# TensorE's attention programs written out without a loop, and two of ScalarE's copies placed ahead of an exponential

## What is computed

```python
x = x + _L0_xattn_ref(_layernorm(x), ctx, ...)   # 8 heads of 128
x = x + _L0_ffn_ref(_layernorm(x), ...)          # ternary mixture of experts
x = x + _L1_xattn_ref(_layernorm(x), ctx, ...)   # 16 heads of 8, with biases
x = x + _L1_ffn_ref(_layernorm(x), ...)
x = x + _L2_xattn_ref(_layernorm(x), ctx, ...)   # 16 heads of 64
x = x + _L2_ffn_ref(_layernorm(x), ...)
x = x + _L3_xattn_ref(_layernorm(x), ctx, ...)   # 16 heads of 64
x = x + _L3_ffn_ref(_layernorm(x), ...)
```

## Time and profile before

| | |
|---|---|
| runs of the kernel, median | 3998.56 us (3996.25 to 4007.36, 3 runs) |
| the profiled execution's own time | 3976.25 us |
| its span, first to last instruction | 3974.5 us |
| mean granted TensorE clock | 0.929 |
| busy: PE, PE's weight loads | 91%, 76% |
| busy: DVE, ACT, POOL | 62%, 46%, 28% |
| DMA queue of kind "instruction" | 305 packets, 5.00 MB |

### The profile page before, as it was taken

One profiled execution on the slowest core, in us unless ns is written; L12 is line 12 of the kernel. 1 busy time (PEld: TensorE's weight loads), 2 busy tenths in 40 slices (PEclk: granted clock), 3 DMA queues, 4 the chain that ended last, 5 costly groups with the idle time before them and its releaser, 6 DMA issues. The chain is left out here.

```text
span 3974.5 us, 110071 instructions
## 1 busy us (share of the span) xinstructions
PE 3612.0 (91%) x44952; PEld 3024.5 (76%) x44952; DVE 2445.7 (62%) x5145; ACT 1821.4 (46%) x3060; POOL 1102.7 (28%) x814
## 2 busy tenths in 40 slices
PE   4999599998989788699999989979999997999999
PEld 3888588886778654488878867768788886888888
DVE  5777555554444499766665657656566665666665
ACT  2555355554444455355555545445455552332322
POOL 1222133334333133222222213312222221222222
PEclk9999799997576599899999989989999998999999
DMA  1000000000000000000000000010000001000000
GB/s 69 11 10 6 25 0 0 0 0 18 9 11 9 8 0 0 23 6 8 6 8 6 6 10 0 0 26 6 9 6 7 8 4 32 1 11 11 0 11 11
DMA packets 14677, 39.22 MB, mean 10 GB/s; under 512 B 3148, under 2 KB 4748, under 8 KB 12813
## 3 DMA queue, kind: packets, MB, share of 16 engines
q1 hardware_dynamic: 14341, 33.97, 2.7%
HBM read 29.77 MB, written 4.19 MB: 9 GB/s over the span
## 5 line engine op out<-in xcount | busy, mean ns | idle before, releaser
L536 ACT ACTIVATE projL<-bank 128x512 f32<-128x512 f32 (+1 forms) x640 | 373.6, 604 | 716.2 <-PE bank L135 700.6
L359 POOL TENSOR_TENSOR probL<-probL,invL 128x1024 f32<-128x1024 f32 x160 | 304.7, 1905 | 1274.2 <-DVE invL L618 1274.2
L1162 POOL TENSOR_TENSOR accM<-accM,partM 128x512 f32<-128x512 f32 x272 | 348.0, 1279 | 817.1 <-DVE partM L1264 815.7
L1235 ACT ACTIVATE siluM<-bank 120x512 f32<-120x512 f32 x240 | 143.7, 599 | 457.3 <-PE bank L135 457.1
L440 PEld LDWEIGHTS bank<-valuesL,probTL 64*64 64x64 f32 x10240 | 282.2, 134 | 69.0 <-issue 54.3
L440 PE MATMUL bank<-valuesL,probTL 64*64 64x128 f32 x10240 | 321.2, 275 | 13.1 <-ACT probTL L546 13.1
L1184 PEld LDWEIGHTS bank<-downT,hM 120*128 120x128 f32 x2560 | 310.5, 192 | 15.0
L615 DVE TENSOR_REDUCE totalL<-probL 128x16 f32<-128x1024 f32 x160 | 194.9, 1218 | 199.4 <-ACT probL L551 199.2
L1184 PE MATMUL bank<-downT,hM 120*128 120x128 f32 x2560 | 311.5, 275 | 0.0
L607 DVE TENSOR_REDUCE neg_maxL<-bank 128x16 f32<-128x1024 f32 x160 | 196.0, 1225 | 186.7 <-PE bank L459 142.4
L1184 PEld LDWEIGHTS bank<-w2T,hM 128*128 128x128 f32 x2304 | 276.1, 192 | 38.5 <-ACT hM L1238 21.6
(11 more groups left out here) (263 smaller groups left out, 8463.4 us busy)
## 6 DMA issues: line engine op xcount, KB each, us to landing
ct0L<-in_ctxP SPq DMA_DIRECT2D x24, 192.0 KB, 2.4
ct1L<-in_ctxP SPq DMA_DIRECT2D x24, 192.0 KB, 3.0
x<-in_x SPq DMA_DIRECT2D x4, 1024.0 KB, 9.0
out<-x SPq DMA_DIRECT2D x4, 1024.0 KB, 3.9
nct<-in_ctxP SPq DMA_DIRECT2D x16, 192.0 KB, 2.4
w_natural<-in_L0w SPq DMA_DIRECT2D x2, 1152.0 KB, 8.9
downT<-in_L3down SPq DMA_DIRECT2D x1, 1200.0 KB, 12.8
gateT<-in_L3gate SPq DMA_DIRECT2D x1, 900.0 KB, 4.8
```

What stands on the lines that cost most here:

```text
L359: nc.gpsimd.tensor_tensor(segments(prob[:, slot, :]), segments(prob[:, slot, :]), per_segment(inv[:, slot, :]), ALU.mult).then_inc(prob_re ...
L536: nc.scalar.activation(proj[:, u, :], rot.bank(step, f"P{u}")[0:rows, :], ACT.Copy, scale=scale if paired and u % 2 == 0 else 1.0).then_in ...
L1162: nc.gpsimd.tensor_tensor(acc[:, :, :], acc[:, :, :], part[:, ex % 2, :, :], ALU.add)\
```

## The change

In both attentions PE's program runs over all 16 groups in Python, so that each group's instructions are written out. ACT, DVE, POOL and SP keep their loops. `wide_attention` serves L0, L2 and L3 alike, so all four attentions of PE lose their loop. In the narrow attention ACT copies the queries and the turned output ahead of the exponentials at `k` = 2.

```diff
@@ wide_attention
+        def straight(group):
+            for j in range(NG):
+                group(j, j % 2)
...
-                sweep_from_two(pe, group)
+                straight(group)
@@ narrow_attention
+        def straight(group):
+            for j in range(NG):
+                group(j, j % 2, (j + 1) // 2 if j + 1 < NG else None)
...
-                groups(pe, group)
+                straight(group)
@@ ACT's group in narrow_attention
+                        if k == 2 and more:
+                            keep_q(i + 1)
+                        if k == 2 and started(i, 1):
+                            keep_output(i - 1)
                         if k or started(i, 1):
                             exponentials(m - 1, (k - 1) % 2)
...
-                        if k == 2 and more:
-                            keep_q(i + 1)
-                        if k == 2 and started(i, 1):
-                            keep_output(i - 1)
```

## The result

| | before | after |
|---|---|---|
| median of the runs | 3997.4 us (3994.05 to 4007.36, 4 runs) | 3833.27 us (3822.01 to 3843.46, 4 runs) |
| the profiled execution's own time, and its span | 3976.25 us, 3974.5 | 3843.46 us, 3841.7 |
| mean granted clock | 0.929 | 0.947 |
| DMA queue of kind "instruction" | 305 packets | 297 packets |

The ratio of the two is 0.9585, with a 95% interval of 0.9547 to 0.9623: 164 us faster.

What follows compares the result with a forecast made beforehand. PE was taken to bound the attentions, through its idle time at jumps and waits and its clock in L1. 3976.25 - 72 - 86 = 3818 us, plus half of the 22 us median gap, gave 3829 us; range 3780 to 3888.

Steps and rivals of the forecast that it cites:

- Term 1: L2 and L3: without PE's jumps back, fetch idle time and the slow work behind it go, -72 us.
- Term 2: L0: its loop shows no fetch to save, and fetching written-out code is hidden: 0, upper bound +3 us.
- Term 3: L1: jump stalls go, waits for the turned output shrink, the clock mostly holds: -86 us.
- the 0.85 that was to show the forecast right: Sign in L1: the stage's granted clock rises from 0.67 to 0.85 or more.
- it holds most of the time: L1's clock: 10 of 13 groups at 19.3 us and 3 at 31.3 make 287 us, 79 less.
- 1.3 at most: L1: PE's waits before the turned probabilities become 1.1 us on average, at most 1.3.
- the first rival: L1: the clock still falls in every group, slow and fast ones alternating; 3878 us, chance 0.22.
- The half of 22 us: Whole kernel: the runs' median lies 22 us above the profiled execution; half was taken, raising 3818 to 3829 us.
- never (3790): Rival, L1: the clock never falls, all 13 groups take 19.3 us; 3790 us, chance 0.2.
- The rival of code that comes too late: All four attentions, L0 first: sequential fetch stalls at packet boundaries, up to 1100 us slower; chance 0.03.

Runs made afterwards that it cites:

- e10: The full change measured again on chip 2, against the kernel before: 3834.6 us, ratio 0.9636.
- e6: The full change, but PE's L0 program is a loop of three turns with four groups (some 2600 instructions): 3882.4 us.
- e7: The full change, but PE's loop of two groups kept in L0; its profiled execution spans 3841.3 us.
- e1: The kernel before with only the wide attentions (L0, L2, L3) written out, L1's loop and ACT's order as before: 3919.8 us, ratio 0.9847.
- e8: e2 plus eight extra matmuls in PE's wait for the turned output in L1: 3796.5 us, ratio 0.9513 to the kernel before.
- e5: The full change plus four extra, overwritten matmuls at k = 3 in L1's groups 1 to 14: 3777.0 us, ratio 0.9506 to the kernel before.
- e2: The full change without the move of ACT's copies (all attentions written out): 3895.3 us, ratio 0.9796 to the kernel before.
- e9: e4 with its two extra matmuls also in group 0: 3774.7 us, ratio 0.9470 to the kernel before.
- e11: e5 measured again beside the full change: 3782.9 us, ratio 0.9500 to the kernel before.
- e4: e5 with two extra matmuls in place of four: 3774.4 us, ratio 0.9452 to the kernel before.

## Why the prediction was right

3829 us was forecast and 3833 measured. That the number is so near is in part luck: two misses cancel. Beside the kernel before on chip 2 the same change gave 147 us (e10) and not 164, where the forecast was 170 below the kernel's median.

**Term 1 held.** 72 us were forecast for L2 and L3, and the timeline shows 31.0 + 41.9 = 72.9. The two parts, idle time and slow work behind it, both went. Nothing became late: eight steps take 459.10 / 6 = 76.5 us, the 76.60 of an undisturbed turn, and DVE is no busier (420.6 us against 420.05 in L2).

**Term 2 held**: 0 was taken, and it is 0 to 0.5 us, within the bound of 3. The reason given (the small body stays on the core, the large one does not) was an inference from packet counts; e6 bears it out. The Trainium skill's rule in "Runtime: NRT & Kernel Launch", Instruction fetch mechanics, is borne out in its kind, a jump back that stalls for the fetch, but not in the two pages of 256 instructions: L0's body of 1300 instructions is far more, and stays. The same section of the Trainium skill, which the prediction read only in part, gives TensorE's instruction memory a size of 2048 instructions. The trace agrees: the body of 1300 that stayed lies below it, and those of L1 (9194 matmuls and 9192 weight loads in 64 steps, some 2300 a turn) and of L2 and L3 (2580) that stalled lie above. No run narrows it down further.

**Term 3 named the right causes and had too large a size.** 86 us were taken for L1. In the profiled executions the 13 groups went from 366.0 to 308.6, which is 57 us and not 79. Group 15 ran at 1.2 GHz in both (25.6 us) and gave nothing of the 7. The stage's clock rose from 0.67 to 0.74 (0.78 in e10), short of the 0.85 that was to show the forecast right. e10 has 296.2, e7 321.2 and e6 338.8 with the same code in L1, so one profile is a draw, and all four lie above the 287 forecast.

The step that failed is "it holds most of the time": "10 of the 13 groups at 19.3 us and 3 at 31.3". In the profile after, three of the 13 groups took 18.8 to 19.1 us, two 31.3 and one 30.8, and the other seven 20.7 to 27.0. The waits were not 1.1 us. The 14.0 / 12 = 1.17 of the profile is a mean of three short ones (0.59 to 0.73 us) and nine of 1.23 to 1.39, all above the 1.12 that had been borne and five of them above the "1.3 at most". Behind six of the nine the clock fell; in e10 behind six of ten of 1.15 to 1.38. The falls did not cost the 12 us a group of the working each time: a group with a fall of 6.8 us in it took 22.1 us, 3 more than a fast one. So the first rival was right that the clock goes on falling, and wrong in what a fall costs.

Nor does the length of a wait decide by itself. In the kernel before one of 1.86 us was borne, which the prediction overlooked when it took 1.12 as the size that the clock has borne; after the change waits of 1.39 us stand on both sides; and in e7 the clock fell behind 1.11. The three rows are from the kernel before (at 2.4 GHz until the jump of 1179), the full change (borne) and e7 (fall at 1096.4):

```profile
1170.14 1.06 PE L809 MATMUL bank<-ident,nprob 128*128 128x128 f32 x8 [1.86 <-ACT oT L976]
...
1162.71 0.98 PE L817 MATMUL bank<-ident,nprob 128*128 128x128 f32 x7 [1.39 <-ACT nprob L980]
...
1096.05 1.68 PE L820 MATMUL bank<-ident,nprob 128*128 128x128 f32 x8 [1.11 <-ACT nprob L983]
```

What else decides whether the clock falls, and for how long, stays open.

**The half of 22 us was too little.** Against the profiled execution the gain was 3976.25 - 3843.46 = 133 us, not 158. Between the medians it was 164. The kernel before was perhaps profiled in an execution whose L1 went well: e1, with the same L1, took 24 us longer there, and among the recorded runs of the kernel before those near 4000 us have a lower clock (0.921) than those near 3976 (0.929 to 0.931). But on chip 2 its median was itself 3977 to 3981 us, and no stage of the other runs was profiled, so where the 22 us came from is not shown. The overestimate of 25 us in the sum (158 against 133) and this underestimate nearly cancel.

**The wait moved as worked out**, from the turned output to the exponentials: 1.06 us was to go per fast group, e8 against e5 shows 1.1, and in group 2 it went from 2.54 us (e2) to 1.39. ACT's exponentials behind the copies did no harm at 1.2 GHz: two whole groups after the change, 1060 to 1121, show PE busy for all 61.00 us.

**The rivals.** The clock falling in every group (3878) and never (3790) enclosed the truth. e5, e9 and e11 show the second case made true by other means: groups of 19.05 us and 3775 to 3783 us in all. The rival of code that comes too late is refuted by L0's 321.5 and 321.1 us written out against 321.05 as a loop, and by L2's steps. (Its "1100 us slower" is what the packets would cost, 312 times 3.6 us; less the gain of 158 it would be some 965.) The advice of the Trainium skill's "TensorE: Matmul & The Clock Gate", Why this matters for your kernels, on how long an idle gap may be, was too lenient for this stage: the clock fell behind gaps of 1.1 to 1.4 us, in e4 behind 0.87 and 0.68, and in e9 behind 0.53 and 0.59.

## What to carry to other kernels

A loop on PE whose body is too large to stay on the core costs a fetch at every jump back (3.1 to 5.0 us idle here, and mostly slow work behind it). Written out, the same code was fetched ahead: no stall was left at these places, and L0 took at most 0.5 us more in 321. Count the instruction packets in a turn of the loop to see which case it is. Where the granted clock is low, look at what stands right ahead of each fall, and how long the clock then stays down: two causes of idle time may each suffice, so that removing one shows little and removing both shows much. A short wait that can't be removed can be filled with wide matmuls whose result is thrown away, which bought 52 to 60 us here on the same chip. And where the clock sets a stage's time, one profile is a draw: take several before a term of a forecast is sized by it.

## What was not expected of the hardware

- In the stage with thin matmuls (32 rows and 64 columns of the array, and products of 9 columns) the clock fell behind idle stretches of 1.1 to 1.4 us, though not behind all of them, once behind 0.87 and 0.68 us (e4), once behind 0.53 and 0.59 (e9) and once behind 0.65 and 0.91 (e10). In L2 it took the stalls of 3.5 us, and behind one of 3.58 (before 1925.21) it did not fall.
- Once at 1.2 GHz it stayed there for between 3 and 133 us in that stage (full change and e7), though PE was busy all the time in the long stretches (61.00 of 61 us in the one above, 132.00 of 132 from 1138 to 1270 in e7). No run shows what brings it back.
- The same code took 296 to 339 us for 13 groups in four profiled executions, by where the clock fell and for how long. The full change's runs spread over 20 us in 3840 (e10), and with the wait filled in groups 0 to 14 (e9) over 8.
